# Layer 0 of a four-layer attention chain: two heads in one stack slot, one in rows 0 to 63 and one in rows 64 to 127

## What is computed

```python
d_head = INNER // HEADS                       # 128 // 8 = 16
qkv = jnp.einsum('oc,bchw->bohw', w_qkv, x)
attn = jnp.einsum('bhdi,bhdj->bhij', q * scale, k)
attn = attn + pos[..., :, None] + pos[..., None, :]
attn = jax.nn.softmax(attn, axis=-1)
y = jnp.einsum('bhij,bhdj->bhdi', attn, v)
y = jnp.einsum('co,bohw->bchw', w_proj, y) + b_proj[None, :, None, None]
z = (x + y).transpose(0, 2, 3, 1)             # then a layer norm over the channels
```

## Time and profile before

| | |
|---|---|
| median of 3 runs | 525.99 us (525.51 to 528.49) |
| profiled execution, its own time | 526.39 us |
| span of the profiled execution, first to last instruction | 524.7 us |
| PE busy | 487.1 us (93%) |
| DVE busy | 361.3 us (69%) |
| ACT busy | 267.1 us (51%) |
| mean granted TensorE clock | 0.977 |

### The profile page before, as it was taken

How to read it: one execution, slowest core, us unless ns; L and a number is a source line. 1 busy time by engine, 2 the same in 40 slices (tenths; PEclk the granted TensorE clock), 3 DMA queues, 4 the chain that set the end, 5 groups by cost and what they waited for, 6 DMA issues and landing times.

```text
span 524.7 us, 7243 instructions
## 1 busy us (share of the span) xinstructions
PE 487.1 (93%) x2388; PEld 247.5 (47%) x2388; DVE 361.3 (69%) x687; ACT 267.1 (51%) x522; POOL 191.7 (37%) x173
## 2 busy tenths in 40 slices
PE   8778999899889997999999999999899999999996
PEld 6435444444236764544444432655444444442463
DVE  7597778878164657887788833738797688862583
ACT  3137667665622423775657663031686665765032
POOL 8200021000000001777677682000586667767000
PEclk9888999999998899999999999998999999999999
DMA  5320431000000053143500000025205410000002
GB/s 142 59 54 17 134 64 33 0 2 2 2 0 1 0 135 79 30 111 90 145 10 3 0 2 2 0 56 116 71 15 122 98 31 2 1 2 1 0 1 80
DMA packets 12101, 22.46 MB, mean 43 GB/s; under 512 B 4391, under 2 KB 5551, under 8 KB 11937
## 3 DMA queue, kind: packets, MB, share of 16 engines
q1 hardware_dynamic: 11088, 21.72, 17.3%
q0 software_dynamic: 832, 0.27, 0.4%
q10 hardware_dynamic: 144, 0.02, 0.0%
HBM read 4.76 MB, written 1.05 MB: 11 GB/s over the span
## 4 chain that ended last, share of the span: by engine, by line
PE 67%; DVE 20%; SPq 5%; issue 3%; ACT 2%; DMA 2%; POOL 0%; ACTq 0%; DVEq 0%; POOLq 0%
PE PV L899 17%; DVE max L634 14%; PE S L888 13%; PE S L861 11%; PE M L916 5%; PE S L1004 4%; SPq L279 3%; PE PV L816 3%; DVE rec_sb L664 2%; PE S L842 2%; PE S L1049 1%; PE PV L842 1%; PE PV L835 1%; PE M L835 1%; SPq L286 1%
## 5 line engine op out<-in xcount | busy, mean ns | idle before, releaser
L634 DVE TENSOR_REDUCE max<-S 128x1 f32<-128x512 f32 x384 | 243.9, 673 | 70.0 <-PE S L861 69.7
L486 ACT ACTIVATE E<-S 128x512 f32<-128x512 f32 x384 | 207.0, 601 | 123.9 <-PE S L888 121.2
L428 POOL TENSOR_TENSOR SUMS<-E 128x512 f32<-128x512 f32 x126 | 159.8, 1281 | 165.2 <-ACT E L486 163.6
L861 PE MATMUL S<-k_stack,q_stack 126*128 126x512 f32 x384 | 175.1, 466 | 4.6 <-DMA k_stack<-kL 2.0
L888 PE MATMUL S<-q_stack,k_stack 128*128 128x512 f32 x384 | 159.8, 423 | 15.6 <-DVE mHL L647 6.3
L861 PEld LDWEIGHTS S<-k_stack,q_stack 126*128 126x128 f32 x384 | 74.7, 195 | 68.3 <-DVE max L634 32.5
L888 PEld LDWEIGHTS S<-q_stack,k_stack 128*128 128x128 f32 x384 | 73.0, 191 | 63.5 <-ACT E L486 23.4
L899 PE MATMUL PV<-E,V 128*32 128x512 f32 x768 | 95.8, 599 | 0.6 <-ACT pv_sb L493 0.6
L664 DVE RECIPROCAL rec_sb<-den_sb 128x64 f32<-128x64 f32 (+1 forms) x54 | 35.8, 668 | 27.6 <-ACT den_sb L503 27.6
L899 PEld LDWEIGHTS PV<-E,V 128*32 128x32 f32 x768 | 20.2, 109 | 45.9 <-issue 36.2
L409 POOL TENSOR_TENSOR att<-pv_sb,rec_sb 128x512 f32<-128x512 f32 x9 | 11.5, 1278 | 65.7 <-DVE rec_sb L664 65.6
(11 more groups left out here) (177 smaller groups left out, 326.5 us busy)
## 6 DMA issues: line engine op xcount, KB each, us to landing
k_stack<-kH SPq DMA_DIRECT2D x32, 128.0 KB, 2.3
q_stack<-qH SPq DMA_DIRECT2D x40, 64.0 KB, 2.0
k_stack<-kL SPq DMA_DIRECT2D x16, 128.0 KB, 2.3
q_stack<-qH SPq DMA_DIRECT2D x16, 128.0 KB, 2.3
q_stack<-mHL SPq DMA_DIRECT2D x96, 2.0 KB
q_stack<-qL SPq DMA_DIRECT2D x20, 64.0 KB, 2.0
X<-x_in_dram SPq DMA_DIRECT2D x2, 512.0 KB, 5.9
k_stack<-kH SPq DMA_DIRECT2D x16, 64.0 KB, 2.4
```

Source lines behind the costliest of these rows:

```text
L428: pool.tensor_tensor(SUMS[:, slot, :], E[:, E_PLAN[s][0], :], E[:, E_PLAN[s + 1][0], :], ALU.add).then_inc(sum_ready, 1)
L486: act.activation(E[:, slot, :], B[:, ring_of_scores(s) % B_RING, :], ACT.Exp, scale=1.0 if l == 0 else float(HEAD_DIM[l]) ** -0.5).then_in ...
L634: dve.tensor_reduce(max8[:, m % 2, r:r + 1], A[:, n % A_RING, :], AX.X, ALU.max, negate=True).then_inc(a_used, 1)
L861: pe.matmul(A[:, n % A_RING, :], q_stack[0:SHIFT_ROW, slot, q0:q0 + P], k_stack[0:SHIFT_ROW, slot, k0:k0 + HALF], start=True, stop=True).t ...
```

## The change

In layer 0 a head now has 64 contraction rows. `slot_of`, `row_of`, `shift_row` and `stack_rows` place it: heads 0 and 1 in rows 0 to 63 of slots 0 and 1, heads 2 and 3 in rows 64 to 127 of the same slots, heads 4 to 7 the same way in slots 2 and 3. A score matmul of layer 0 reads 64 rows and one for the maxima 62. The unit whose maxima are taken is two units ahead, which is always a head of the other half, so neighbouring matmuls of the two kinds use opposite halves of the rows. No slot is used twice in layer 0. Layers 1 and 2 keep their stacks; since rows 96 to 127 are no longer zero after layer 0, POOL clears them in `q_stack` between the layers, and SP and TensorE wait for that.

```diff
-        def slot_of(h):
-            return h % SLOTS
+        def slot_of(l, h):
+            return h % SLOTS if l else 2 * (h // 4) + h % 2
+
+        def row_of(l, h):
+            return 0 if l else ROW_TILE * (h % 4 // 2)
+
+        def shift_row(l, h):
+            return row_of(l, h) + (P if l else ROW_TILE) - 2
+
+        def stack_rows(l, h, shifted):
+            return slice(row_of(l, h), shift_row(l, h) + (2 if shifted else 0))
...
+                if l == 1:
+                    sp.wait_ge(stacks_clear, 4)
                 shift_rows(l, 0)
...
-                    if h >= SLOTS:
+                    if l and h >= SLOTS:
                         sp.wait_ge(b_done, STEPS * l + 32 + TILES * (h - SLOTS + 1))
...
-            for dst, r in ((q_stack, p0), (k_stack, p0 + 2), (k_stack, SHIFT_ROW)):
+            for dst, r in ((q_stack, p0), (k_stack, p0 + 2), (k_stack, ROW_TILE - 2), (q_stack, ROW_TILE + p0),
+                           (k_stack, ROW_TILE + p0 + 2), (k_stack, P - 2)):
                 pool.dma_start(dst[r:r + 2, :, :].bitcast(F32), ones[0:2 * SLOTS * N // P, :]).then_inc(one_rows_in, 16)
...
-            def load_pos(h):
-
-                pool.wait_ge(b_done, 32 + TILES * (h - SLOTS + 1))
+            for tile in range(2):
                 for part, src in enumerate((posH, posL)):
+                    if tile == 0:
+                        pool.wait_ge(pos_ready, part + 1)
                     for dst, r in ((q_stack, p0 + 2 + part), (k_stack, p0 + part)):
-                        pool.dma_start(dst[r:r + 1, slot_of(h), :].bitcast(F32), src[h:h + 1, :]).then_inc(pos_late[h - SLOTS], 16)
+                        row = ROW_TILE * tile + r
+                        pool.dma_start(dst[row:row + 1, 0:HEADS_B, :].bitcast(F32),
+                                       src[HEADS_B * tile:HEADS_B * (tile + 1), :]).then_inc(pos_rows[tile], 16)
...
+                    pool.wait_ge(b_done, STEPS)
+                    pool.wait_ge(att_ready, BLOCKS - 1)
+                    pool.memset(q_stack[3 * DP:P, :, :].bitcast(F32), 0.0).then_inc(stacks_clear, 1)
+                    pool.wait_ge(stacks_clear, 4)
...
-                pe.matmul(A[:, n % A_RING, :], q_stack[0:SHIFT_ROW, slot, q0:q0 + P],
-                          k_stack[0:SHIFT_ROW, slot, k0:k0 + HALF], start=True, stop=True).then_inc(a_done, 1)
+                pe.matmul(A[:, n % A_RING, :], q_stack[rows, slot, q0:q0 + P],
+                          k_stack[rows, slot, k0:k0 + HALF], start=True, stop=True).then_inc(a_done, 1)
...
-                pe.matmul(B[:, ring_of_scores(s) % B_RING, :], k_stack[:, slot, P * t:P * (t + 1)],
-                          q_stack[:, slot, HALF * f:HALF * (f + 1)],
+                pe.matmul(B[:, ring_of_scores(s) % B_RING, :], k_stack[rows, slot, P * t:P * (t + 1)],
+                          q_stack[rows, slot, HALF * f:HALF * (f + 1)],
                           start=True, stop=True).then_inc(b_done, 1)
```

More of the change, by code:

```diff
@@ L33 @@
 POS_ROWS = 4
-SHIFT_ROW = P - 2
+ROW_TILE = P // 2
 NORM_GROUP = 8
@@ L171, in attention_chain @@
         pool_chain, dve_chain = sem("pool_chain"), sem("dve_chain")
-        pos_late = [sem(f"pos_late{i}") for i in range(NH - SLOTS)]
-        pos_ready, pos_rows, one_rows_in = sem("pos_ready"), sem("pos_rows"), sem("one_rows_in")
+        pos_ready, one_rows_in = sem("pos_ready"), sem("one_rows_in")
+        pos_rows = [sem(f"pos_rows{i}") for i in range(2)]
         xn_ready = sem("xn_ready")
@@ L413, in _ @@
                 if l == 0:
-                    for h in range(SLOTS, NH):
-                        load_pos(h)
                     for b in range(BLOCKS - 1):
                         normalise(l, b)
+                    pool.wait_ge(b_done, STEPS)
+                    pool.wait_ge(att_ready, BLOCKS - 1)
+                    pool.memset(q_stack[3 * DP:P, :, :].bitcast(F32), 0.0).then_inc(stacks_clear, 1)
+                    pool.wait_ge(stacks_clear, 4)
                     continue
@@ L850, in scores_for_max @@
                 _, _, g, f, h = unit_of(j)
-                n, slot = STEPS * l + i, slot_of(h)
+                n, slot, rows = STEPS * l + i, slot_of(l, h), stack_rows(l, h, False)
                 if r == 0:
@@ L883, in scores @@
                 _, _, _, f, h = unit_of(j)
-                m, slot = UNITS_L * l + j, slot_of(h)
+                m, slot, rows = UNITS_L * l + j, slot_of(l, h), stack_rows(l, h, True)
                 if t == 0:
@@ L1127 @@
     row3 = np.concatenate([g[f"L3_conv_b{n}"] for n in "qksv"])[None, :]
+    pos_order = [4 * (i % 4 // 2) + 2 * (i // 4) + i % 2 for i in range(NH)]
     arrays = {"x_in_dram": g["x"].reshape(KC, P, N), "w0_dram": w0, "w1_dram": w1, "w2_dram": w2, "w3_dram": w3,
-              "pos_dram": g["L0_conv_pos_bias"], "cols_dram": cols, "row3_dram": row3}
+              "pos_dram": np.ascontiguousarray(g["L0_conv_pos_bias"][:, pos_order]), "cols_dram": cols, "row3_dram": row3}
     nc = bacc.Bacc("TRN2", target_bir_lowering=False, num_devices=1)
```

25 lines of the change are left out of this document (11 added, 14 removed).

## The result

The changed kernel takes 546.7 us (median of 4 runs, 538.67 to 548.72) against 525.75 us for the kernel before (median of 4), 4% between the medians. The ratio is 1.031 with a 95% interval of 1.020 to 1.042. The profiled execution took 545.54 us, its span is 543.8 us. The times of the four runs follow their granted clocks: 0.934 in the run of 538.67 us, 0.911 in that of 548.72 us; in the profiled execution before, it was 0.977.

A forecast was written before the change was run, and what follows sets the result against it. It took VectorE's waits for TensorE at layer 0's 11 value groups as the bound. Terms -2.4 (overlap), -0.2 (slow stretch), +0.2 (start) sum to -2.4 us: 523.6 us, own range 522.4 to 524.9, with other cases 521.0 to 527.8.

The forecast's parts named there:

- The clock falls in layer 0: Rival, chance 0.12: TensorE stands still longer, values' units run at 1.2 GHz, 2.4 us each; three make 530.8 us.
- The overlap: Layer 0, before the values: neighbouring opposite-half matmuls run together, saving 0.24 us in 9 units, 0.12 in 2; 2.4 us.
- More than one pass: Rival, chance 0.14: half-height matmuls also deliver sooner, 0.47 instead of 0.24 us saved in 11 places; 521.0 us.
- nothing overlaps: Rival, chance 0.18: the two kinds of matmul still run one after the other, leaving only the later start; 526.2 us.
- units with a gathering: Layer 0, 2 of 11 units, gathering of sums after the first score matmul: only the last two overlap, 0.12 us saved each.
- The transposes: Layer 0: the next matmul may wait for the full-height transpose's 0.27 us; VectorE's buffered maxima cover it, cost nothing.
- The change of shape: Rival, chance 0.07: switching matmul height at transposes drains TensorE; at 0.5 us, 14 lose 0.3 each, 527.8 us.
- The start: Before the first score matmul: three more DMAs of ones on POOL delay position rows; 0.2 us lost, bounds 0 and 1.2.
- The clearing: Between layers 0 and 1, on POOL: takes 4.39 us (low end 1.1), hidden by 36 us of cover; cost 0.
- waits gone: Layer 0: heads 5 to 7 load earlier, but no score matmul there waited for a load; gain 0.
- The slow stretch at 41 us: Layer 0, 41.44 to 43.17 us at 1.2 GHz: overlap brings a matmul forward; 0.2 us saved, bounds 0 and 0.4.

The follow-up runs named there:

- same-half pair: Stretch of a separate test kernel: two half-height matmuls a step on the same rows, at VectorE's pace; recorded busy 6.00 of 6 us, yet its clock fell.
- pace kernel: Separate kernel without the chain: seven stretches of 40 steps, one or two score-like matmuls per VectorE maximum (about 0.6 us), dense full-height matmuls ahead of each; ran once.
- kernel without overlap: Changed kernel with heads dealt out so that neighbouring score matmuls mostly use the same half of the rows: 553.1 us, ratio 1.054 (1.047 to 1.060).
- full pair: Stretch of a separate test kernel: two full-height matmuls a step at VectorE's pace; recorded busy 23.00 of 23 us, its clock didn't fall.

## Why the prediction was wrong

- **Which case came.** "The clock falls in layer 0" had 0.12, and it is what happened; the forecast's sum took the clock as unchanged, and that is the step that failed. The prediction had the right doubt in hand (matmuls of half height had not been seen at all) and gave it too little weight: the change halves what the array works on in every step of layer 0, and the trace held a pace of one matmul at 0.50. It put the cause down to standing still, about 0.24 us more for each of a unit's eight pairs. Against one matmul a step at 0.50 it also set the same pace at 1.00 between 195 and 200 us; in the pace kernel one full matmul a step shows 1.00 too over 143 to 148 us, close behind dense matmuls, and 0.50 over 151 to 165. VectorE's maxima waited 22.3 us between 56 and 133 us, not about 13. The same-half pair and the kernel without overlap showed that half height is enough for the fall.
- **Its size.** The rival priced a unit at 1.2 GHz at 2.4 us and took three of them. A unit at the lowered clock took 68.21 - 59.53 = 8.68 us, 2.1 more than the 6.57 at the full one: the price was about right, the number was not. Six of the twelve groups of values took over 3.2 us, and behind them the tail, which the prediction never costed, lost 6.0 us more (148.15 to 172.20 takes 24.0 us, against 18.0 before).
- **The overlap.** Right to 0.01 us in a plain unit: 0.25 saved, 6.57 for the forecast 6.6; VectorE's wait 1.31 for 1.55. "More than one pass" and "nothing overlaps" are out. In the units with a gathering the sum took 0.12 saved; 0.14 to 0.16 was lost. Its 2.4 us would have been 9 x 0.24 - 2 x 0.15 = 1.9.
- **The transposes.** Right: the matmul behind one starts 0.17 us later than before, the prediction had allowed 0.24, and VectorE doesn't wait.
- **The change of shape.** It costs 0.2 us at a transpose, where the slack hides it. Whether it is what the gathering units lose was not tested; with 0.42 us each way it is dear only where it stands in every step.
- **The start.** Taken as 0.2 lost with a bound of 1.2; measured 3.7 at the first score matmul. Two things were missed. VectorE's copy seems held until POOL's issues and its clearing of V are through (it ends 0.5 us behind the clearing in both kernels: 12.16 and 11.66, 14.24 and 13.74, and took 2.03 us again when the issues were moved), so that all that hangs on it starts 2.1 us late. And SP's own issues of the loads get slower beside the added transfers. The prediction had looked at POOL's queue alone. How the 3.7 us divide between the two is not measured.
- **The clearing, waits gone.** 4.36 us for 4.4, hidden, and no gain from the earlier loads: right.
- **The slow stretch at 41 us.** 0.2 saved was expected; the clock was 0.50 from 30 to 56 us instead, and the term was swallowed.
- **Its sums.** Two come out slightly otherwise from its own terms: the forecast's own range at 522.6 to 525.2, not 522.4 to 524.9, and "more than one pass" at 521.1. Neither matters here.

## What to carry to other kernels

Packing two matmuls side by side in the array gives back time only where TensorE is waited for, and takes work away from the array everywhere: before packing in a kernel that runs at VectorE's pace, look whether the granted clock is 1.00 because of the very work that is to be halved, and give that case its full price. A saving of 0.24 us a unit stood against 2.1 us a unit at 1.2 GHz. Useless matmuls give part of such a loss back, but at 1.2 GHz they lengthen the steps themselves. Transfers and clearings on POOL's queue are not free when they stand behind nobody: see which VectorE copies and which other queue's issues run beside them.

## What the runs showed of the hardware

- The recorded busy time of TensorE doesn't foretell the clock: at 6.00 us busy of 6 (57 to 63 us) the half pair on the same rows still had 1.00, and then 0.50 with 23.00 of 23; the full pair kept 1.00 with 23.00 of 23.
- A VectorE copy of 8 x 32 elements took 2.03 us beside POOL's clearing of V, 4.10 beside three more issues of transfers and the clearing. The Trainium skill, "SBUF — State Buffer", section "SBUF: two separate sides", says that one shared pair of ports is an exclusive lock and not a split bandwidth: it goes for a whole instruction to whichever starts first, a GpSimd instruction or a VectorE one in a two-port mode (or, against one that reads SBUF, with two inputs there). That the copies end behind the clearing (12.16 and 14.24) would fit a lock. But the copy of the changed kernel is recorded as starting at 10.14, ahead of the clearing at 11.92, and ended behind it all the same, which that rule doesn't explain; what held it was not tested by itself.
- DMAs on POOL's queue slow SP's issues beside them: 2.31 for 1.30 us beside three of two rows, and 1.95 for 0.87 beside four of one row in each of four slots. Whether the queue or the memory is the place stays open.
- Between the starts of a half-height and a full-height matmul stand 0.42 us at full clock, against 0.23 to 0.34 between pairs of one height. The Trainium skill, "TensorEngine Tiling (Array Packing)", section "Key Properties", says that a change of the tiling mode drains TensorE; it gives no figure, and the trace agrees.
